# A two-layer graph network on one core: TensorE signals through a drain behind each group of matmuls

## The reference

```
h = relu(layernorm(x))                                  # 3125 x 256
ZU = einsum('nd,kdr->knr', h, U)                        # 4 heads x 16
logits = (ZU[:, src] * ZU[:, dst]).sum(-1) / 4          # one per edge and head
alpha = softmax of logits over the edges of one target
agg = segment_sum(alpha * ZU[:, src], dst)
Z_half = 0.5 * h + 0.5 * (agg weighted by softmax(head_w), times U)
x = x + relu(Z_half + 0.1 * residual @ Dmat - 0.05)     # first layer
h = relu(layernorm(x))
red = segment_sum(h[src] + relvectors[edge_rel], dst)
out = x + gru_cell(red, h, w_ih, w_hh, b_ih, b_hh)      # second layer
```

## Time and profile before

| | us |
|---|---|
| median of 3 runs | 1061.32 |
| lowest and highest | 1059.81 and 1064.99 |
| span of the profiled execution | 1059.6 |
| busy in it: PE, PEld | 862.7, 640.4 |
| busy in it: DVE, ACT, POOL | 631.8, 421.5, 647.8 |
| first gather of the first layer begins | 46.87 |
| last gather begins | 722.93 |

### The profile page before, as it was taken

How to read it: one execution, slowest core, us unless ns; L and a number is a source line. 1 busy time by engine, 2 the same in 40 slices (tenths; PEclk the granted TensorE clock), 3 DMA queues, 4 the chain that set the end, 5 groups by cost and what they waited for, 6 DMA issues and landing times.

```text
span 1059.6 us, 14242 instructions
## 1 busy us (share of the span) xinstructions
PE 862.7 (81%) x4828; PEld 640.4 (60%) x4828; DVE 631.8 (60%) x1285; ACT 421.5 (40%) x804; POOL 647.8 (61%) x969
## 2 busy tenths in 40 slices
PE   6943688787788878787887786676999999999996
PEld 6741676565566656565665564464676676677773
DVE  5340577787888867777777764453243343388853
ACT  5423216555555555555565543341211111124441
POOL 4698888888888888888888888883001001000000
PEclk9996557787777777777787787787999999999998
DMA  9361334445455544554454553323344434421111
GB/s 196 77 156 36 74 78 120 119 119 125 116 128 130 132 123 112 129 123 125 119 129 111 120 124 89 88 51 84 95 126 141 124 116 137 124 87 49 50 51 34
DMA packets 54646, 112.99 MB, mean 107 GB/s; under 512 B 15435, under 2 KB 32968, under 8 KB 51443
## 3 DMA queue, kind: packets, MB, share of 16 engines
q1 hardware_dynamic: 34632, 81.38, 24.1%
q0 software_dynamic: 18880, 30.57, 17.5%
q10 hardware_dynamic: 1056, 0.07, 0.1%
HBM read 80.99 MB, written 30.86 MB: 106 GB/s over the span
## 4 chain that ended last, share of the span: by engine, by line
POOL 57%; PE 31%; issue 7%; DVE 2%; DMA 1%; SPq 1%; ACT 1%; POOLq 0%; DVEq 0%; ACTq 0%
POOL shared L724 28%; POOL cnt_rows L729 15%; POOL zs_third L724 13%; PE bank L1948 13%; PE bank L1947 6%; PE bank L1974 5%; PE bank L1975 2%; PE bank L1925 1%; PE bank L1875 1%; PE bank L1707 1%; PE bank L1971 1%; PE bank L1966 1%; DMA xs<-in_x 0%; DVE bst L885 0%; SPq L471 0%
## 5 line engine op out<-in xcount | busy, mean ns | idle before, releaser
L724 POOL DMA_INDIRECT shared<-zu_table,src_col x306 | 300.0, 980 | 51.6 <-issue 48.7
L729 POOL MEMSET cnt_rows<- 54x300 f32 x450 | 165.5, 368 | 0.3
L724 POOL DMA_INDIRECT zs_third<-zu_table,src_col x144 | 140.8, 978 | 23.0 <-issue 23.0
L999 DVE TENSOR_TENSOR setup<-iota_b,bank 128x500 bf16<-128x500 bf16 (+1 forms) x252 | 140.0, 609 | 1.1 <-PE bank L1911 0.5
L1570 ACT ACTIVATE setup<-bank 125x500 bf16<-125x500 f32 (+1 forms) x126 | 81.2, 681 | 106.5 <-PE bank L1911 70.7
L1804 PEld LDWEIGHTS bank<-zus,shared 125*128 125x128 f32 x900 | 114.0, 209 | 15.5 <-issue 14.9
L1804 PE MATMUL bank<-zus,shared 125*128 125x64 f32 x900 | 115.6, 292 | 7.8 <-ACT shared L1515 5.9
L1829 PE MATMUL bank<-layer,oh 128*125 128x84 f32 x900 | 110.1, 284 | 0.0
L1829 PEld LDWEIGHTS bank<-layer,oh 128*125 128x125 f32 x900 | 107.7, 200 | 0.1
L1911 PE MATMUL bank<-setup 128*125 128x125 bf16 x450 | 58.3, 279 | 52.0 <-DVE setup L999 42.9
L1911 PEld LDWEIGHTS bank<-setup 128*125 128x125 bf16 x450 | 48.4, 184 | 78.2 <-DVE setup L999 70.7
(11 more groups left out here) (235 smaller groups left out, 1775.8 us busy)
## 6 DMA issues: line engine op xcount, KB each, us to landing
shared<-in_edges SPq DMA_DIRECT2D x25, 1125.0 KB
counts_table<-setup SPq DMA_DIRECT2D x18, 683.6 KB
own_table<-own_out SPq DMA_DIRECT2D x25, 375.0 KB
shared<-own_table SPq DMA_DIRECT2D x25, 375.0 KB
zus<-counts_table POOLq DMA_DIRECT2D x9, 683.6 KB, 5.2
shared<-counts_table POOLq DMA_DIRECT2D x9, 683.6 KB, 5.0
shared<-zu_table,src_col POOLq DMA_INDIRECT x306
h_table<-h2s SPq DMA_DIRECT2D x25, 125.0 KB
```

What stands on the lines that cost most here:

```text
L724: nc.gpsimd.indirect_dma_start(out=zs[t % 3][:, j * KR:(j + 1) * KR], out_offset=None, in_=zu_table, in_offset=bass.IndirectOffsetOnAxis(a ...
L729: nc.gpsimd.memset(idle, 0.0).then_inc(idle_set, 1)
L999: nc.vector.tensor_tensor(chunk[n % 2][:, 0:(b - a) * W].rearrange("p (g w) -> p g w", w=W), io, ps(3, 128, at + a, at + b).unsqueeze(2).b ...
```

## The change

In the first layer the last matmul of a group no longer counts the semaphore. Behind the group TensorE executes a `drain`, an instruction that waits until the matmuls before it have ended, and the drain counts the semaphore. This is done in `turn_logits`, `turn_most`, the sum over edges in `attend`, `turn_own`, `own_products`, `turn_row`, `turn_means`, `add_means` and each of the seven groups of `count_ahead`. `target_rows` had three semaphores `zd_made[c]`, one per chunk; it now has one, `zd_made`, counted by one drain behind all 18 matmuls, so VectorE's first two chunks of `logits` wait for all of them. A window with counts has 16 drains, one without has 9 (8 in the first, where `turn_own` and `own_products` have nothing to do yet, and the last). GpSimd's memsets, all matmuls and their order, and the second layer's `gru` are as before.

```
-        zd_made = [sem(f"zd_made{c}") for c in range(3)]
+        zd_made = sem("zd_made")
...
-                dve.wait_ge(zd_made[c], t + 1)
+                dve.wait_ge(zd_made, t + 1)
...
                     for j in range(a, b):
-                        last = mm(ps(c, 128, (j - a) * KR, (j - a + 1) * KR), ohT[:, j * 128:(j + 1) * 128],
-                                  zus[:, t, :], start=True, stop=True)
-                    last.then_inc(zd_made[c], 1)
+                        mm(ps(c, 128, (j - a) * KR, (j - a + 1) * KR), ohT[:, j * 128:(j + 1) * 128],
+                           zus[:, t, :], start=True, stop=True)
+                pe.drain(fusable=False).then_inc(zd_made, 1)
...
-                tr(ps(4, 128, 0, K * C), segmax[:, :], ident[0:K * C, 0:K * C]).then_inc(mT_made, 1)
+                tr(ps(4, 128, 0, K * C), segmax[:, :], ident[0:K * C, 0:K * C])
+                pe.drain(fusable=False).then_inc(mT_made, 1)
...
-                last.then_inc(agg_made, 1)
+                pe.drain(fusable=False).then_inc(agg_made, 1)
...
-                last.then_inc(own_made, 1)
+                pe.drain(fusable=False).then_inc(own_made, 1)
...
-                last.then_inc(counts_ahead, 1)
+                pe.drain(fusable=False).then_inc(counts_ahead, 1)
```

More of the change, by code:

```diff
@@ L734, in windowed @@
                 each_window(source_rows)
-                pool.wait_ge(zd_made[2], NW)
+                pool.wait_ge(zd_made, NW)
                 pool.wait_ge(st_counts, 32 * AHEAD)
@@ L1510, in target_one_hots @@
                 if t:
-                    act.wait_ge(zd_made[2], t)
+                    act.wait_ge(zd_made, t)
                 away = dst_bc[h].bitcast(fp32)
@@ L1810, in turn_logits @@
                 for s in range(3):
-                    last = tr(ps(3, K * C, s * 128, (s + 1) * 128), L[:, s:s + C, :].rearrange("p j k -> p (j k)"), ident[:, :])
-                last.then_inc(LT_made, 1)
+                    tr(ps(3, K * C, s * 128, (s + 1) * 128), L[:, s:s + C, :].rearrange("p j k -> p (j k)"), ident[:, :])
+                pe.drain(fusable=False).then_inc(LT_made, 1)
             def turn_most(t):
                 pe.wait_ge(segmax_made, t + 1)
-                tr(ps(4, 128, 0, K * C), segmax[:, :], ident[0:K * C, 0:K * C]).then_inc(mT_made, 1)
+                tr(ps(4, 128, 0, K * C), segmax[:, :], ident[0:K * C, 0:K * C])
+                pe.drain(fusable=False).then_inc(mT_made, 1)
             def attend(t, h, ahead):
@@ L1828, in attend @@
                 for j in range(C):
-                    last = mm(ps(5, W, 0, SUMS), oh[:, h, j * W:(j + 1) * W], V[:, j, :], start=j == 0, stop=j == C - 1)
-                last.then_inc(agg_made, 1)
+                    mm(ps(5, W, 0, SUMS), oh[:, h, j * W:(j + 1) * W], V[:, j, :], start=j == 0, stop=j == C - 1)
+                pe.drain(fusable=False).then_inc(agg_made, 1)
                 if t:
@@ L1859, in turn_own @@
                 for c in range(CH):
-                    last = tr(ps(7, 128, c * W, (c + 1) * W), h2s[:, t % 2, c * 128:(c + 1) * 128], ident[0:W, 0:W])
-                last.then_inc(own_turned, 1)
+                    tr(ps(7, 128, c * W, (c + 1) * W), h2s[:, t % 2, c * 128:(c + 1) * 128], ident[0:W, 0:W])
+                pe.drain(fusable=False).then_inc(own_turned, 1)
             def own_products(t):
@@ L1875, in own_products @@
                     mm(ps(7, W, 0, 2 * D), rows, whhT[:, c, 0:2 * D], start=False, stop=c == CH - 1)
-                    last = mm(ps(2, W, 0, D), rows, whhT[:, c, 2 * D:3 * D], start=False, stop=c == CH - 1)
-                last.then_inc(own_made, 1)
+                    mm(ps(2, W, 0, D), rows, whhT[:, c, 2 * D:3 * D], start=False, stop=c == CH - 1)
+                pe.drain(fusable=False).then_inc(own_made, 1)
             def turn_row(t):
@@ L1881, in turn_row @@
                 for c in range(CH):
-                    last = tr(ps(5, 128, c * W, (c + 1) * W), hrow[:, c * 128:(c + 1) * 128], ident[0:W, 0:W])
-                last.then_inc(hrow_turned, 1)
+                    tr(ps(5, 128, c * W, (c + 1) * W), hrow[:, c * 128:(c + 1) * 128], ident[0:W, 0:W])
+                pe.drain(fusable=False).then_inc(hrow_turned, 1)
             def dense_part(t):
@@ L1896, in turn_means @@
                 pe.wait_ge(means_made, 2 * t + 2)
-                tr(ps(4, PACK, 0, W), means[:, :], ident[0:W, 0:W]).then_inc(turned_made, 1)
+                tr(ps(4, PACK, 0, W), means[:, :], ident[0:W, 0:W])
+                pe.drain(fusable=False).then_inc(turned_made, 1)
             def add_means(t):
                 pe.wait_ge(meansT_made, t + 1)
-                mm(ps(6, W, 0, D), meansT[0:KR, :], UV[:, :], start=False, stop=True).then_inc(grad_made, 1)
+                mm(ps(6, W, 0, D), meansT[0:KR, :], UV[:, :], start=False, stop=True)
+                pe.drain(fusable=False).then_inc(grad_made, 1)
             def count_ahead(t, g):
@@ L1910, in count_ahead @@
                 for k in range(b - a):
-                    last = mm(ps(g % 2, W, k * W, (k + 1) * W), low_chunk[n % 2][:, k * W:(k + 1) * W],
+                    mm(ps(g % 2, W, k * W, (k + 1) * W), low_chunk[n % 2][:, k * W:(k + 1) * W],
                               key_chunk[n % 2][:, k * W:(k + 1) * W], start=True, stop=True)
-                last.then_inc(counts_ahead, 1)
+                pe.drain(fusable=False).then_inc(counts_ahead, 1)
             def count_pairs(t, g):
```

## The result

The changed kernel takes 1089.74 us (median of 4 runs, 1089.07 to 1091.97), the kernel before 1061.90 (1059.81 to 1064.99). The ratio is 1.0269, 95% interval [1.0244, 1.0295]. I had forecast 1063.5 and a range of 1059 to 1081: slower was given 0.42, but the time lies outside the range. The experiments ran in five groups, each on a chip of its own and at one time; the kernel before took between 1059.5 and 1101.9 us in them, and a kernel is read against the runs of before in its own group. Runs more than 1.5% above the fastest of the same kernel are left out of medians and ratios.

What follows compares the result with a forecast made beforehand. The prediction took GpSimd's gathers to bound the first layer and matmuls the second; the loop's added time was free, so 1059.6 plus 2.0 for the tail plus 1.7 for the median gave 1063.3, stated as 1063.5, range 1059 to 1081.

Steps and rivals of the forecast that it cites:

- The two limits: First layer: lag of 21 us by window 15 and 25 by 19 fits reserves of 28.0 and 49.3; gathers undelayed.
- rival B: First layer: breaks exceed 1.9 us a window, GpSimd waits for V_made; at 2.5 a window, 1073.5 us; chance 0.33.
- The loop's term, 1.4 us a window: First-layer window loop: drains add 1.24 us on TensorE's chain plus 0.2 for target_rows, with ends 0.3 and 3.6.
- the breaks: TensorE's chain from counts 2 to counts 5: overlap lost across drains, with the signal, costs 1.24 us a window.
- the other half: VectorE's part of the window: drains of turn_logits, counts 0 and 1, turn_means and the edge sum are hidden.
- the merged signal: target_rows: one signal instead of three, pushed by the breaks before it, costs some 0.2 us a window.
- The limit of 1.9 us a window: First-layer loop: beyond this added time, each further 0.1 us delays the gathers by about 1.7 us.
- The drain's price: One break in a running TensorE stream: 0.35 us at half clock, 0.30 at full; signal alone 0.05.
- The tail: Work behind the last gather: seven breaks and four signals add 2.0 us, from 0.5 to at most 4.
- C: First-layer loop: gaps behind drains keep TensorE's clock low, 28.8 us a window, 1087 us; chance 0.07.
- D: GpSimd's gathers: the shifted loop makes them faster, 6 us might come back, 1057 us; chance 0.04.
- E: Whole kernel: drains only make signals 0.05 us later, the tail costs 0.5, 1061.8 us; chance 0.10.

Runs made afterwards that it cites:

- e3: Kernel before with counting drains only behind count_ahead's seven groups in windows 1 to 18, and one target_rows signal: 1069.87 us, ratio 1.0072.
- h3: Kernel before with non-counting drains in windows 0 to 18 alone and one target_rows signal, fourth chip: 1059.54 us, ratio 0.9994.
- e2: Kernel before without drains, only the three target_rows semaphores merged into one, counted by the last matmul: 1061.81 us, ratio 1.0002.
- h4: Kernel before with non-counting drains in windows 19 to 24 alone and one target_rows signal, fourth chip: 1064.17 us, ratio 1.0038.
- h2: Kernel before with non-counting drains only behind turn_most, add_means, turn_row, own_products and counts 2 to 6, one target_rows signal: 1059.55 us, ratio 1.0003.
- h1: Kernel before with non-counting drains only behind seven groups predicted hidden by VectorE's work, one target_rows signal: 1059.99 us, ratio 0.9999.
- e1: Changed kernel with its drains kept but counting nothing; each group's last matmul counts the semaphore, one target_rows signal: 1089.10 us, ratio 1.0265.
- f5: Changed kernel with all 351 drains behind matmuls that count, and target_rows counting its three chunks separately again: 1092.77 us, ratio 1.0287.
- f6: Changed kernel with matmuls counting, one target_rows signal, and each of the 351 drains replaced by a nop: 1061.17 us, ratio 0.9994.
- f8: Kernel before with non-counting drains in windows 0 to 18 alone and one target_rows signal, third chip: 1116.62 us, ratio 1.0147.
- f9: Kernel before with non-counting drains in windows 19 to 24 alone and one target_rows signal, third chip: 1112.03 us, ratio 1.0017.
- e4: Kernel before with counting drains behind all groups except count_ahead, nine a window in all windows: 1082.53 us, ratio 1.0171.
- f3: Kernel before without GpSimd's memset behind each of its 450 gathers: 1386.77 us, ratio 1.3051.
- f4: Changed kernel without GpSimd's memset behind each of its 450 gathers: 1462.16 us, ratio 1.3773.
- k1: The changed kernel, unaltered, run once more on a fifth chip: 1120.51 us, ratio 1.0157.
- g1: Kernel before with GpSimd's memset behind each gather half as long, 150 columns instead of 300: 1331.09 us, ratio 1.2011.

## Why the prediction was wrong

**The step that failed** is in "The two limits": "By window 19 the lag is 25 us, within the 49.3 us of waits." Both halves of it were wrong. The lag at window 19 is 45.4 us, and VectorE's waits for the gathers, of which 42.7 us lie in windows 19 to 24, are not a reserve of 49.3. While VectorE waited, TensorE's own work of those windows went on. When the gathers no longer hold them back, windows 19 to 24 take 108.3 us together in the changed kernel, against 124.1 before: 15.8 us are given back, and 29.6 of the 45.4 stay. Neither error alone would have done it. With the lag of 25 and the reserve of 15.8 the forecast would have been 1063.5 + 9 = 1073; with the loop as measured and the reserve of 49.3 it would have been rival B with 1063.5 + 11 = 1074. Both are inside the range.

The reserve is no fixed number either. The smallest time of these five windows is 99.6 (e3), a reserve of 24.5. Single windows from 20 on show what it hangs on (h3, then e2, neither with a drain there):

```profile
642.75:662.38 19.63, 17.59 (x99) 12.96 (x98) 12.39 (x26) 9.47 (x18) 17.39 (x28) 0.85 0.49 116
...
643.23:666.46 23.23, 17.44 (x98) 12.96 (x97) 12.46 (x27) 9.69 (x18) 20.82 (x32) 0.79 0.44 105
```

e2 takes 23.2, 23.7 and 22.9 us for windows 20 to 22 without a drain, no less than the changed kernel (23.6, 23.6, 23.7); h3, where results are on time, takes 19.6 and 17.6 for the first two. In h3 the lag of 18.4 us at window 19 is gone by window 22. So in the group with punctual results the step held, for a lag of that size.

**The loop's term, 1.4 us a window, was mis-sized: it measured 2.54** (28.11 less 25.57). Where drains are punctual, the breaks cost 0.98 (h3 against h4) where I had 1.24, they lie where I put them (h2), and the other half is hidden (h1). So much of the mechanism was right. Of the 0.2 for the merged signal nothing was found. The remaining 1.56 of the 2.54 is a term that the prediction put at nothing without a reason, though rows of 8.3, 7.7 and 7.2 us ended by "remote" stood in the trace of before: it comes where results of TensorE are late, 2.3 us a window of late drains in the changed kernel, 0.02 in h3.

How much of the 1.56 is the drains' doing is open. Within a group, one trace each, they make the loop longer by 1.16 (e1 against e2), 1.70 (f5 against f6), 0.06 (f8 against f9) and 0.98 us (h3 against h4). No run tests that, and f8 against f9 speaks against it as a general rule. What e1 against e2 shows is that the last windows take up the lag that the kernel has without drains (15 us), but not the 23 us that the drains put on top of it.

**The limit of 1.9 us a window held.** Against the trace of before e3's loop is 1.72 longer, and its last gather comes at 722.6 as before; e4's is 2.12 longer, and it comes at 727.7. Beyond the limit I gave GpSimd 17 us per us: (2.54 - 1.9) x 17 = 10.9; the last gather of the changed kernel came 13.0 us later. Rival B so happened as described, with its price (1073.5) too small, since it left the last windows' lag out for the same reason as the forecast. As a sum: 2.2 before window 2, 17 x 0.98 = 16.7 for breaks, 17 x 1.56 = 26.5 for the rest of the loop, less 15.8 given back, makes 29.6 at window 24. The 0.98 in it is from another chip than the 2.54.

**The drain's price.** Row by row it was near. In the changed kernel the drain ends 0.02 behind the last matmul (I had 0.05), and the next load starts 0.05 behind it without a wait, 0.18 behind one semaphore wait and 0.29 behind two. Breaks in a stream measured from start to start: counts 2 to `turn_most` 0.11 to 0.40 (+0.29; I had 0.35), `own_products` to counts 5 +0.40 (0.30), counts 5 to 6 +0.39. Two that I had taken as nearly fresh starts cost more: behind `add_means` +0.25 (0.12), before L1871 +0.30 (0.15).

**The tail.** I had 2.0. h4, where the gathers set window 24 as before (733.5), has a ratio of 1.0038, 4.0 us (2.5 to 5.5), twice as much and at the end of my bounds. In the traces 328.9 us follow window 24 in h4 and 325.4 in h3, 3.4 more; in the changed kernel it is 0.7 more than before.

**The clock** (C): 0.76 against 0.77 over 178 to 610 us; e1 had 0.79 and the whole loss. Refuted. The Trainium skill, "TensorE: Matmul & The Clock Gate", section "A second HAM failure mode: psum-queue depth-cycling", which the prediction names, reports such idles, and throughput lost to them, of another kernel. That this speaks against breaks of the kind tried here was my conclusion from it, and the clock of the runs does not bear it out. **D** and **E** did not happen.

## What to carry to other kernels

An engine's waits in a stretch are not a reserve of their full length: ask what the other engines in the loop need once the wait is gone, and take the shortest window that the trace shows. In this kernel a drain cost nothing where a slower engine covered it, and 0.25 to 0.40 us in a stream. A wait whose releaser the profile cannot name, on a program of one core, is worth a question even at 8 us: in f3 the same row had 287 us. Compare a pair of kernels in one group of runs before a difference between groups is put down to the change.

## What was not expected of the hardware

- TensorE's work is held up while GpSimd's indirect gathers follow each other fast. In the sum over edges the drain ends 18.0 to 18.7 us late with no memset between gathers (f4, a gather every 1.25 us). With one every 1.48 us it is up to 1.9 us late in the first result and up to 4.6 in k1. In g1, with one every 1.35 us, VectorE waits 8.2 us on average for that result. In f3 the matmuls follow each other in multiples of 0.70 us instead of 0.11. What is shared between the two was not found: neither whether GpSimd's issuing or the transfers do it, nor whether a pause of another kind than a memset would do as well, was run.
- It differs between the groups: none late in one, 2.3 us a window in the first result and 2.5 to 3.3 in four groups. Each chip was used at one time only, so that a property of the chip and one of the moment are not told apart.
- A nop costs nothing there: 351 of them, ratio 0.9994.
- In single windows the clock stood at 0.62 or 0.63, and they are 3 to 6 us longer: k1 has one of 29.3 us with TensorE busy 23.5, where its neighbours take 20.8 to 25.2. None of windows 19 to 24 of the first result is among them.
